# Second attention: two maxima between a head group's shift and its transposes, and five instead of ten maxima ahead of the first exponential

## The reference

```python
xq, xk, xv = (x @ wq.T), (x @ wk.T), (x @ wv.T)      # 32 heads of 16
xq, xk = rotary_pos_emb(xq), rotary_pos_emb(xk)
scores = jnp.einsum('bqhd,bkhd->bhqk', xq, xk) * scale
scores = jnp.where(causal[None, None], scores, NEG_INF)
probs = jax.nn.softmax(scores, axis=-1)
out = jnp.einsum('bhqk,bkhd->bqhd', probs, xv).reshape(B, T, C)
return out @ wo.T
```

## Time and profile before

| what | value |
|---|---|
| median of three runs | 1244.46 us (1243.29 to 1249.1) |
| profiled execution, its own time | 1242.31 us |
| its span, first to last instruction | 1240.5 us |
| TensorE busy | 1152.3 us, 93% of the span |
| VectorE busy | 866.3 us, 70% |
| ScalarE busy | 352.7 us, 28% |
| GpSimd busy | 147.9 us, 12% |
| mean granted TensorE clock | 0.971 of full |
| chain that ended last | 80% TensorE, 9% VectorE, 4% DMA |

### The profile page before, as it was taken

How to read it: one execution, slowest core, us unless ns; L and a number is a source line. 1 busy time by engine, 2 the same in 40 slices (tenths; PEclk the granted TensorE clock), 3 DMA queues, 4 the chain that set the end, 5 groups by cost and what they waited for, 6 DMA issues and landing times.

```text
span 1240.5 us, 28148 instructions
## 1 busy us (share of the span) xinstructions
PE 1152.3 (93%) x9930; PEld 521.7 (42%) x9930; DVE 866.3 (70%) x2483; ACT 352.7 (28%) x746; POOL 147.9 (12%) x223
## 2 busy tenths in 40 slices
PE   6799987999999999899899999999979899999992
PEld 3478563443333333444344444444624333333330
DVE  5832675877777774578889999942458678777754
ACT  5444610001010101322176777784110010101010
POOL 2220011011010101344000000000110010101010
PEclk9899979999999999999999999999899999999996
DMA  9100433158723436418704333006741655616566
GB/s 359 59 2 1 158 137 130 37 184 287 259 98 96 167 124 211 180 62 180 170 3 87 53 53 53 2 2 251 301 177 36 246 176 189 216 36 215 168 204 251
DMA packets 63668, 174.33 MB, mean 141 GB/s; under 512 B 9885, under 2 KB 16627, under 8 KB 61351
## 3 DMA queue, kind: packets, MB, share of 16 engines
q1 hardware_dynamic: 55471, 150.60, 37.5%
q0 software_dynamic: 5760, 18.88, 4.3%
q10 hardware_dynamic: 2296, 3.05, 0.7%
HBM read 785.47 MB, written 22.03 MB: 651 GB/s over the span
## 4 chain that ended last, share of the span: by engine, by line
PE 80%; DVE 9%; DMA 4%; issue 2%; ACT 2%; SPq 1%; POOL 0%; POOLq 0%; ACTq 0%; DVEq 0%
PE PS L1123 30%; PE PS L1142 14%; PE PS L1648 6%; PE PS L1635 5%; PE PS L1613 5%; PE PS L837 3%; PE PS L822 2%; PE PS L1675 2%; PE PS L1563 2%; PE PS L602 2%; DVE PS L1771 2%; PE PS L1568 1%; PE PS L586 1%; PE PS L1638 1%; DMA HH<-in_w 1%
## 5 line engine op out<-in xcount | busy, mean ns | idle before, releaser
L1123 PE MATMUL PS<-arena 128*32 128x400 f32 x3456 | 397.4, 502 | 8.1 <-DMA HH<-in_w 4.2
L1123 PE MATMUL PS<-HH,arena 128*32 128x400 f32 x1152 | 396.7, 502 | 0.0
L1123 PEld LDWEIGHTS PS<-arena 128*32 128x32 f32 x3456 | 147.3, 111 | 246.9 <-issue 238.8
L1313 DVE STREAM_TRANSPOSE arena<-arena 32x192 f32<-32x192 f32 x576 | 211.4, 367 | 7.2
L1771 DVE CUSTOM_DVE_ANT_0 PS<-PS,U 128x128 f32<-128x128 f32 (+7 forms) x256 | 186.7, 786 | 15.4 <-PE PS L1613 15.0
L1142 PE MATMUL PS<-arena 128*32 128x512 f32 x1512 | 192.3, 592 | 4.0 <-DVE arena L1313 4.0
L1291 DVE STREAM_TRANSPOSE arena<-arena 32x128 f32<-32x128 f32 x544 | 164.7, 303 | 16.7 <-DMA arena<-h_scratch,RT 8.8
L1718 ACT ACTIVATE arena<-PS 128x512 f32<-128x512 f32 (+3 forms) x384 | 160.1, 512 | 54.9 <-PE PS L1638 48.2
L1196 ACT ACTIVATE arena<-PS 128x400 f32<-128x400 f32 x72 | 36.2, 504 | 422.3 <-PE PS L1123 422.2
L1297 DVE TENSOR_TENSOR arena<-arena,PS 128x400 f32<-128x400 f32 x72 | 40.9, 571 | 128.6 <-ACT arena L1196 128.5
L1123 PEld LDWEIGHTS PS<-HH,arena 128*32 128x32 f32 x1152 | 126.1, 111 | 0.0
(11 more groups left out here) (258 smaller groups left out, 1253.2 us busy)
## 6 DMA issues: line engine op xcount, KB each, us to landing
arena<-in_w SPq DMA_DIRECT2D x456, 800.0 KB
arena<-in_w2a SPq DMA_DIRECT2D x266, 768.0 KB
HH<-in_w SPq DMA_DIRECT2D x152, 800.0 KB
HH<-in_w2a SPq DMA_DIRECT2D x38, 768.0 KB
arena<-split_scratch SPq DMA_DIRECT2D x96, 128.0 KB, 6.3
arena<-y_scratch SPq DMA_DIRECT2D x24, 256.0 KB, 5.3
split_scratch<-arena SPq DMA_DIRECT2D x8, 768.0 KB, 4.8
arena<-in_wqkv SPq DMA_DIRECT2D x3, 1024.0 KB, 6.3
```

Of the source, the lines that this page charges most:

```text
L1123: mm = eng.matmul(PS[SR * j:SR * j + SR, 2 * hf + m, 0:FH], XBT[:, u, c, SR * j:SR * j + SR], W13[j][:, c // 2, m, c % 2, hf * FH:(hf + 1) ...
L1313: tr = eng.transpose(ACT_T[SR * b:SR * b + SR, u, :, rows], src[:, :, SR * b:SR * b + SR])
```

## The change

Three things are edited in `plan_attn1`. In the list of maxima, mtr of group g - 1 moves behind the first two maxima of group g, so the order is now: maxima of a group, its shift, two maxima of the next group, then mtr. After the last group nothing stands between. `ahead` goes from 44 to 39 units: all 32 maxima of group 0 with shift and mtr, and five instead of ten maxima of group 1. The three strings of `GROUP1` are replaced, so the interleaving of maxima, exponentials, avs, copies and turns in the loop is another. No instruction is added or taken away.

```diff
--- before.py
+++ after.py
@@ -1350,12 +1350,12 @@
 
 
         GROUP1 = (
-            ("mememeaemeemecemeaemmemmeeeameeemeemeemeatcamemem"
-             "emmaemeemeemeaaeeemmmeememmaaemeemeeteeememaaemem"),
-            ("emememeemceameemaemmeemmemeameeemeeemeaacmmeeteme"
-             "tememeeaemeemeemeeamaememmeemmeammaeeememeeaameem"),
-            ("mmemeeecmmeeaeeemeameeemeaeeeeememmmcaameeeemtaee"
-             "eeameemmmmtmeemaemeemmmmeeeemmeaaemmemeeemeeemaam"),
+            ("meemeeameemmaememeemeemceeemeeemtaamememmemeecaem"
+             "emeameeemmaamemeememeemeemeaameememmeeemmeteaamee"),
+            ("emeemeemeeaemmecemmeemaemeeemeeemamemeemmemaamcee"
+             "meemammeememmeeteetemeemeemaamameememeeemmeaaamee"),
+            ("emeeeemcaemeemeeemtemmmmamemememmememmemeeeemceaa"
+             "aeeeemeamaeemmmeemmemetmaeemeeemeeaaeememeememeaa"),
         )
 
         def plan_attn1():
@@ -1381,9 +1381,12 @@
 
             maxima = []
             for g in range(NG):
-                maxima += [("max", g, h, i) for h in range(GH) for i in range(NT)] + [("shift", g), ("mtr", g)]
-
-            ahead = GH * NT + 2 + 10
+                of_group = [("max", g, h, i) for h in range(GH) for i in range(NT)]
+                between = 2 if g else 0
+                maxima += of_group[:between] + [("mtr", g - 1)] * (g > 0) + of_group[between:] + [("shift", g)]
+            maxima.append(("mtr", NG - 1))
+
+            ahead = GH * NT + 2 + 5
             front = [((n - ahead) / ahead, u) for n, u in enumerate(maxima[:ahead]) if u[0] != "max" or u[1:3] > (0, 0) or u[3] >= 6]
             for w in range(11, 16):
                 at = (w - 16) / 5.0
```

## The result

The changed kernel took 1252.83 us (median of 12 runs, 1248.68 to 1260.44) against 1245.26 us for the kernel before on the same chip (12 runs, 1241.53 to 1249.13): ratio 1.006, interval 1.0043 to 1.0077. It is slower by 0.6%. The forecast of 1247.0 us had allowed 1244 to 1250 for its own case, so it is 5.8 us short, and the side is not the forecast one (no change within 0.5%). The wider range, to 1254, holds the time only because the slower rival's 1253.3 had been taken into it; the mechanism of that rival is not what happened, so this is luck.

What follows compares the result with a forecast made beforehand. TensorE was taken to bound the loop, VectorE the stretch ahead. Front -2.9, group 0 +1.1, groups 1 to 5 +2.3, group 6 +2.3, group 7 -0.4: with rounding +2.5 us on the 1244.46 median, 1247.0 us, range 1240 to 1254.

Steps and rivals of the forecast that it cites:

- the slower rival: Second attention's loop: the rival "VectorE's chain sets the period", +8.8 us to 1253.3 us, chance 0.13.
- the front: Ahead of the loop: five maxima fewer before the first exponential, which comes at 620.15 for 623.05; gain 2.9 us (2.2 to 3.3).
- the mechanism of the groups: Loop groups 1 to 5: 4.2 us of TensorE work against 5.25 needed, so 1.1 us wait at each first exponential.
- The hop: From a group's transposes through copy and four SP-issued DMAs to the next group's first exponential: 5.25 us (4.95 to 5.45).
- No wait at the transposes: Loop, TensorE: the shift is done 0.3 us ahead of the transposes' place; gain 0.2 us in groups 1 to 5.
- The sum for group 0: First group of the loop: -0.1 - 0.15 + 1.35 (wait at the next first exponential) = +1.1 us.
- groups 1 to 5: Loop: -0.2 (shift's wait) - 0.44 (fewer av blocks) + 1.1 (wait at the exponential) = +0.46 us each, +2.3 together.
- Group 6: Loop: +1.36 (3072 more columns streamed) - 0.22 (av blocks) + 1.2 (wait at the exponential) = +2.3 us.
- VectorE's chain sets the period: Rival, loop: cycle of exponential, maxima, shift, transposes and transfer, 29.1 us plus gaps, paces groups; 1253.3 us, chance 0.13.
- No wait: Rival, first exponential of each group: the 8.0 us of waits go and -5.5 remain; 1239.0 us, chance 0.13.
- The front gives nothing: Rival, ahead of the loop: wider spacing of maxima and late start eat the 2.9 us; +5.4, 1249.9 us, chance 0.08.
- Exponentials ahead of their buffer: Loop: three exponentials of step (1,5) precede the av freeing ScalarE's buffer; covered by 2.7 us of avs, cost nothing.

Runs made afterwards that it cites:

- two between alone: Kernel before with two maxima of the next group between a group's shift and its transposes, old strings and ten maxima ahead kept: 1242.48 us, ratio 0.9979.
- the wait filled: Changed kernel with eight extra unread matmuls on TensorE just ahead of the wait for group 0's first exponential: 1251.43 us, ratio 1.0036.
- nothing between: Changed kernel with the two maxima between shift and transposes taken out, new strings and five maxima ahead kept: 1247.53 us, ratio 0.9994.
- two queues: Changed kernel with the shift rows of heads 2 and 3 issued from ScalarE's queue, heads 0 and 1 staying on SyncE's: 1245.33 us, ratio 0.9988.
- seven issues: Kernel before with the rows of three of four heads sent in halves, seven DMA issues on SyncE's queue for four: 1248.45 us, ratio 1.0015.
- five issues: Changed kernel with the first head's rows sent in two halves, five DMA issues on SyncE's queue for four: 1263.17 us, ratio 1.0147.
- the table early: Changed kernel with ScalarE's exponential table loaded ahead of the loop by one exponential of a single column: 1250.53 us, ratio 1.0028.
- two between and the table early: Kernel before with two maxima between shift and transposes, and ScalarE's exponential table loaded ahead of the loop: 1240.97 us (6 runs), ratio 0.9939.
- five ahead alone: Kernel before with five instead of ten maxima ahead of the first exponential, old strings and order kept: 1291.57 us, ratio 1.0354.
- new strings and ten ahead: Changed kernel with ten instead of five maxima ahead of the first exponential, new strings and two maxima between kept: 1277.33 us, ratio 1.0251.

## Why the prediction was right or wrong

**Right: the front.** Forecast -2.9 us, measured -2.76. With the changed order and four issues on one queue it is 39.09 to 39.32 us in five profiles; with the order of before it is 40.84 to 42.54 in three, so the gain is 1.5 to 3.4 us (1.5 to 2.8 without the 42.54, which has a stretch at half clock). The forecast laid all of it to the five maxima. The profiles divide it otherwise: two between alone, with ten ahead, already has a front 1.0 us shorter (40.84 us), and from ten to five ahead with the new strings it is 1.7 us (40.79 to 39.11). The start of the loop "near 620" missed in absolute time only because that execution was late ahead of the attention.

**Right: the mechanism of the groups.** The idle at each group's first exponential, ended by a DMA, was forecast at 1.1 us start to start and is 1.2. The hop was put at 5.25 us (4.95 to 5.45) and is 5.41. Longer hop, shorter hop and longer distance each moved the groups by what the rule says, within 0.1 us. "No wait at the transposes" held too, bar 0.09 us.

**Missed: the granted clock.** No case asked what idle time on TensorE costs afterwards. The sum for group 0 was +1.1 us; it is +4.60. Without the half-clock stretch it would be some 31.0 us (31.10 with the wait filled, 30.98 with nothing between), so the stretch is 3.1 us, almost half of what the sum lacks. The step that failed stands in the front's term: "TensorE's own work from the transposes is about 3.5 us, so it waits there". By the prediction's own times that is a new wait of 5.4 - 3.5 = 1.9 us ahead of group 0's first exponential (measured 1.83), and nothing was put for what comes behind it. (The 1.35 us in group 0's sum is the next wait, ahead of group 1; the clock stayed at 1.00 behind that one in the changed kernel.) Whether the clock falls in a given group was not to be had from the profile of before: with nothing between it stayed at 1.00 in spite of idle times of 2.16, 0.80 and 1.10 us, and with two queues it fell behind 1.08, 0.84 and 1.10. The plan of before is not free of it either: behind its wait of 2.63 us at the transposes of group 0 the clock stayed at 1.00 in its profile and fell to 0.50 in that of seven issues. What decides is open.

**Missed in size: groups 1 to 5.** Forecast +0.46 us each, measured 0.93 to 1.01, so +4.9 us in all for +2.3. The hop is 0.16 us longer than taken. The other 0.4 us a group were put at nothing: TensorE's waits for score banks, 70 to 100 ns at each of four places a group and some smaller ones (0.1 us a group in the kernel before), and the 0.09 us at the transposes. I had counted av blocks in the new strings, but not compared when each maximum's bank comes free.

**Missed in size: the rest.** The wait ahead of group 1 is 1.80 us for 1.35, because the hop there is 5.74 us. Group 6 gained +2.54 us for +2.3, group 7 -0.13 for -0.4. From the first maximum to the last turn the sum was +2.4 us, and measured is 276.85 - 267.70 = +9.15. The 6.75 between them are 3.1 for the clock, 2.6 in groups 1 to 5, 0.4 for group 0's longer wait and 0.65 in group 6, group 7 and the front.

**The rivals.** *VectorE's chain sets the period* named the right time (1253.3 us) and groups over 30.3, for a reason that the runs exclude. Its sign, maxima back to back from the first exponential to the shift, is not there: VectorE stands idle for TensorE early in the group (1.51 us, then the row below) and is back to back only from 694.75 on. The shift is done 0.75 us before the transposes start, and the chain, where it does close, has a period of 29.69 us (the prediction's 29.1 without gaps, and 0.6 of them for the 1.6 that the rival needed). It was close: 0.6 us from deciding. A right number from a wrong mechanism would have led to work on VectorE, where nothing is to be gained at 30.3. *No wait* came to life only when its premise was built, with two queues. *The front gives nothing* is out, though its sign, a first exponential after 622, came true (623.50): counted from the first maximum it is 2.76 us earlier.

```profile
688.67 0.97 DVE L1774 CUSTOM_DVE_ANT_0 PS<-PS,U 128x768 f32<-128x768 f32 x1 [1.18 <-PE PS L1616]
```

**Exponentials ahead of their buffer**: costed at nothing, and no wait of TensorE at that place appears.

## What to carry to other kernels

When a reordering shortens the lead of a transfer's consumer, write down need and distance for every place, and charge need less distance to the bottleneck engine; slack of 2.8 us made three more issues free here in six groups of seven, and without slack one more issue cost its full 0.69 us a group. An order list and its lead are one setting: here the new list with the old lead cost 30 us over the kernel before, and the new lead with the old list 45 us. New idle on TensorE should be priced twice, once as idle and once as the risk of a stretch at 1.2 GHz behind it; single waits of 1.5 us and more, and several of about 1 us close together, are the places to look.

## What the runs showed of the hardware

**The landing of small transfers.** From the start of the last of n issues on one queue to the matmul that waits for it, with the issues evenly spaced in the row: four issues, 714.11 + 3 x 0.69 = 716.17 to 718.17, 2.00 us; five, 684.13 + 4 x 0.69 = 686.88 to 688.88, 2.00; seven, 827.03 + 6 x 0.68 = 831.10 to 833.09, 1.99. The first issue takes a little longer than the others, and by the single issues in the traces (716.23, 686.94, 831.13) it is 1.94, 1.94 and 1.96 us. So the hop here is 1.35 us (transposes, copy, hand-over) + 0.69 us per issue but the last + 2.0 us. The Trainium skill, "DMA: Bandwidth & Descriptors", section "Anatomy of one DMA", puts the fixed cost of one DMA at about 2.0 us, fitted on GpSimd's path. These rows, on SyncE's queue, agree for the last one (1.94 to 2.00 us), and add that the ones ahead of it on the queue are paid one after the other.

**Two queues.** With two issues each on SyncE's and ScalarE's queues, the last two start at 714.76 (ScalarE's) and 714.79 (SyncE's) and the exponential at 717.09: 2.3 us, not 2.0. Halving the row of issues saved 1.0 us of the 1.38.

**Clock.** The granted clock fell from 1.00 to 0.50 in ten of the fourteen profiles, counted between the first maximum and the last turn. For 6.8 us: behind waits of 1.83 and 1.09 us (the changed kernel, twice; with five issues the first was 2.49), and behind three of 0.84 to 1.10 us with some work between (two queues). For 3.4 us: behind single waits of 1.82 (the table early), 1.65 (the first wait filled), 1.76 (five issues, group 2), 1.95 (two between and the table early), 2.16 (five ahead alone) and 2.63 us (before with seven issues), and three times with new strings and ten ahead. The one of 2.63 us, at the transposes of group 0:

```profile
618.36 1.01 PE L1621 MATMUL PS<-identb,arena 128*12 128x128 bf16 x8 [2.63 <-DVE arena L1781]
```

```profile
616.00:618.00 2.00, 0.00 (x0) 0.00 (x0) 1.83 (x7) 0.00 (x0) 0.00 (x0) 1.00 0.00 0
618.00:620.00 2.00, 1.64 (x9) 1.26 (x10) 0.80 (x2) 0.00 (x0) 0.00 (x0) 0.51 0.04 8
```

It doesn't follow from the idle time alone: the same 2.63 us left the clock at 1.00 in the kernel before; the wait ahead of group 1 (1.8 us start to start, 1.65 idle) brought it down with the first wait filled, and not in the changed kernel; and with five issues waits of 1.7 to 2.2 us ahead of six other groups did not. Waits of 1.2 us once every 30 us, in groups 2 to 6, never did.
